# The last output store of a fused FFN kernel: waited for behind the block's end barrier, and issued in two halves from two engines

## The chip, the cores and the metric

The kernel runs on one core of one Trainium2 chip. Its time is the device time of one execution in microseconds; lower is better. The profile is a hardware trace of one execution, and its "span" runs from the first to the last recorded instruction of the program.

## What is computed

For eight images x of 1024 x 512 (float32) a reaction-diffusion step gives y, and y goes through a feed-forward layer whose two weight matrices get a per-image rank-structured addition:

```python
du_dt = zX * lap_x(y) + zY * lap_y(y) + zR * y * (1 - y)          # per image
h   = einsum('bsd,hd->bsh', du_dt, W1) + scale * einsum('bsd,bhd->bsh', du_dt, m1) + b1
h   = gelu(h)
out = x + einsum('bsh,oh->bso', h, W2) + scale * einsum('bsh,boh->bso', h, m2) + b2
```

Here m1 and m2 are outer products of rows 1 to 16 of du_dt of that image. There are B = 8 images, S = 1024 rows, D = 512 input and output channels, and 2048 hidden channels. The output is 8 x 1024 x 512 float32, 16.8 MB.

## The kernel before

The work of an image b is two halves h of 512 rows. A half accumulates its second layer in four PSUM banks `po[0]` to `po[3]`, each 128 rows x 512 channels, over 16 hidden tiles. `layer2_late` (L638 to L640 are its matmuls) finishes the four banks one after the other for the last hidden tile, i = 7, and signals each with `s_l2L`.

`ev(b, h, t)` (L1348) on VectorE adds bank `po[t]` to `xr[:, t, :]`, which holds x + b2, and signals `s_ev`. `store_out(b, h, t)` (L341) on SyncE waits for that and stores the 128 x 512 tile (256 KB) to `out`; its landing adds 16 to the semaphore `d_o[t]`. The `xr` buffer is loaded again for the next half only when `d_o[0]` to `d_o[3]` have arrived.

For the last half of the last image (b = 7, h = 1) nothing follows. VectorE ends with

```python
            c21(B - 1, 7)
            glL(B - 1, 1, 7)
            for t in range(4):
                ev(B - 1, 1, t)
```

and SyncE ends with

```python
            for t in range(4):
                store_out(B - 1, 1, t)
            for t in range(4):
                e.wait_ge(d_o[t], 16 * 2 * B)
```

The last wait (L495) is inside the block, so that the barrier of the block's end starts only when the last store has landed. TensorE ends with `layer2_late(7, 1, 7)`, ScalarE with `ghL(7, 1, 7)` (L929), and GpSimd with the transfer that adds b2 into `xr` (L539).

Of the kernel before, what the change touches and what calls it, by code (L numbers as in the profile page):

```python
# [5 lines left out]
def adaln_ffn_kernel(nc: bass.Bass, xT, xs, x, xn, pk, w1, w2, b2, out):  # L6
# [3 lines left out]
    ALU = mybir.AluOpType  # L10
    ACT = mybir.ActivationFunctionType

    B, S, D = 8, 1024, 512
# [5 lines left out]
    ctx = ExitStack()  # L19
    with ctx:  # L20
        def sb(name, shape, dt=f32):
            return ctx.enter_context(nc.sbuf_tensor(name, shape, dt))

        def sems(names):
            return [ctx.enter_context(nc.semaphore(n)) for n in names.split()]
# [28 lines left out]
        xr = sb("xr", [128, 4, 512])  # L54
# [8 lines left out]
        po = [ctx.enter_context(nc.psum_tensor(f"po{t}", [128, 512], f32)) for t in range(4)]  # L63
# [16 lines left out]
        s_l2E, s_l2L = sems("s_l2E s_l2L")  # L80
# [4 lines left out]
        s_w2f, s_w2h, s_w2l, s_ev, s_scal, s_sc = sems("s_w2f s_w2h s_w2l s_ev s_scal s_sc")  # L85
# [11 lines left out]
        d_U, d_V, d_o = sems("d_U0 d_U1"), sems("d_V0 d_V1"), sems("d_o0 d_o1 d_o2 d_o3")  # L97
# [18 lines left out]
        def steps(b, h, i):  # L116
            return 16 * b + 8 * h + i + 1

        def late(b, h, i, t=0):
            return 22 * b + 11 * h + i + t + 1  # L120
# [22 lines left out]
        def evs(b, h, t):  # L143
            return 8 * b + 4 * h + t + 1
# [80 lines left out]
        def bank_of(b, h, i, lt):  # L225
            if h == 0:
                return ph[i % 2 if lt else 2 + i % 2]
            return ph[i % 4 if lt else (i + 2) % 4]

        block = ctx.enter_context(nc.Block())  # L230

        @block.sync
        def _(e):
            def load_X(b, n):
                if (b, n) > (1, 0):
                    pb, pn = (b, n - 1) if n else (b - 1, 7)
                    e.wait_ge(s_mul, at_mul(pb, pn))
                    e.wait_ge(s_mt, at_sum(pb, pn))
                e.dma_start(X[:, :, :].rearrange("p r s -> p (r s)"), xT[b, n]).then_inc(d_x[8], 16)
# [99 lines left out]
            def store_out(b, h, t):  # L339
                e.wait_ge(s_ev, evs(b, h, t))  # L340
                e.dma_start(out[b, 512 * h + 128 * t:512 * h + 128 * t + 128, :], xr[:, t, :]).then_inc(d_o[t], 16)  # L341
# [73 lines left out]
            for b in range(1, B):  # L415
# [69 lines left out]
                if b + 1 < B:  # L485
# [3 lines left out]
                    load_EB2(b + 1, 1)  # L489
                    if b + 2 < B:  # L490
                        load_X(b + 2, 2)
            for t in range(4):
                store_out(B - 1, 1, t)
            for t in range(4):
                e.wait_ge(d_o[t], 16 * 2 * B)  # L495

        @block.gpsimd
        def _(e):
# [279 lines left out]
        def _(e):  # L778
# [128 lines left out]
            def gelu_L(b, h, i):  # L907
                bank, k = bank_of(b, h, i, 1), tile_of(b, h, i, 1)
                if h == 0:
                    e.wait_ge(s_p3, pairs(b, i))  # L910
                elif b == 0:
                    e.wait_ge(s_p4, i + 1)
                else:
                    e.wait_ge(s_c21, strassen(b, i))
                e.activation(bank[:, :], bank[:, :], ACT.Gelu, bias=b1t[:, k:k + 1]).then_inc(s_actL, 1)  # L915
# [8 lines left out]
            def ghL(b, h, i):  # L924
                if h or b == 0 and i:
                    pb, p_h, pi, t = (b, h, i - 1, 0) if i else (b, 0, 7, 3)
                    e.wait_ge(s_l2L, late(pb, p_h, pi, t))
                e.wait_ge(s_actL, steps(b, h, i))
                e.activation(gh[:, 1, :], bank_of(b, h, i, 1)[:, :], ACT.Copy).then_inc(s_ghL, 1)  # L929
# [216 lines left out]
                    outer(b + 1, 2)  # L1146
            gelu_L(B - 1, 1, 7)
            ghL(B - 1, 1, 7)

        @block.vector  # L1150
        def _(e):
# [176 lines left out]
            def c21(b, i):  # L1328
                e.wait_ge(d_U[i % 2], half_of(b, i))
                e.wait_ge(s_p4, pairs(b, i))  # L1330
                Z_ = ph[i % 4]
                e.tensor_tensor(Z_[:, :], Z_[:, :], UVs[:, 1 + i % 2, :], ALU.add).then_inc(s_c21, 1)  # L1332
# [6 lines left out]
            def glL(b, h, i):  # L1339
                e.wait_ge(s_ghL, steps(b, h, i))  # L1340
                e.tensor_tensor(gl[:, 1, :], bank_of(b, h, i, 1)[:, :], gh[:, 1, :].bitcast(f32),  # L1341
                                ALU.subtract).then_inc(s_glL, 1)

            def ev(b, h, t):
                if t == 0:
                    e.wait_ge(d_xa, 16 * (2 * b + h + 1))
                e.wait_ge(s_l2L, late(b, h, 7, t))
                e.tensor_tensor(xr[:, t, :], po[t][:, :], xr[:, t, :], ALU.add).then_inc(s_ev, 1)  # L1348
# [258 lines left out]
                        mul(b + 2, (i - 4) // 2)  # L1607
            c21(B - 1, 7)
            glL(B - 1, 1, 7)
            for t in range(4):  # L1610
                ev(B - 1, 1, t)

_INS = ["xT", "xs", "x", "xn", "pk", "w1", "w2", "b2"]
# [41 lines left out]
```

## Time and profile before

| | |
|---|---|
| median of 3 runs | 1337.73 us (1337.72 to 1338.11) |
| the profiled execution's own time | 1337.8 us |
| its span | 1335.6 us |
| own time minus span | 2.2 us |
| TensorE busy | 1330.8 us of the span |
| granted TensorE clock | 1.000 |
| last matmul starts | 1331.57 us |
| last addition ends | 1332.69 us |
| last DMA-queue issue of a store starts | 1332.7 us |
| last instruction (barrier release) | 1335.6 us |

The span is covered by TensorE almost from end to end; the change touches only the last four microseconds of it. An engine's name with a q (SPq, ACTq, POOLq) is its instruction sequencer: DMA issues, semaphore waits and the barrier's instructions stand there. A store's row gives how long its issue took; "DMA to landing" is the time from the issue to the semaphore's arrival.

### The profile page before, as it was taken

What the parts mean: (1) busy time and instruction counts of PE and PEld (TensorE: products, weight loads), DVE (VectorE), ACT (ScalarE), POOL (GpSimd) and SP (SyncE); (2) the same over time, 40 slices, a digit from 0 to 9 for tenths busy, and PEclk for the clock granted to TensorE, in tenths of its full rate; (3) what the DMA queues carried; (4) which work ended last, traced back from release to release, by engine and by line L of the source; (5) the groups of instructions that cost most, each with busy time, mean ns of one, the idle gap of its engine ahead of it and who ended that gap; (6) DMA issues with size and microseconds to landing.
All of it is one profiled execution on the core that took longest, in us unless ns stands there. A gap on an engine that the chain in (4) does not pass through costs nothing.

```text
span 1335.6 us, 17133 instructions
## 1 busy us (share of the span) xinstructions
PE 1330.8 (100%) x5904; PEld 1100.7 (82%) x5904; DVE 1034.6 (77%) x1775; ACT 795.1 (60%) x1376; POOL 256.5 (19%) x258
## 2 busy tenths in 40 slices
PE   9999999999999999999999999999999999999998
PEld 7888888888888888888888888888888888888887
DVE  8878799858897688976899668996689957665343
ACT  7644567645775556754677546675467754666442
POOL 1000122301232012320132201331022310232000
PEclk9999999999999999999999999999999999999999
DMA  7764388777777577876768667786767866776661
GB/s 245 194 155 151 80 206 213 202 214 204 185 207 200 184 213 198 208 192 200 206 189 221 181 219 191 194 218 182 222 177 215 209 183 200 162 193 162 173 196 48
DMA packets 140069, 253.51 MB, mean 190 GB/s; under 512 B 13648, under 2 KB 37456, under 8 KB 139984
## 3 DMA queue, kind: packets, MB, share of 16 engines
q1 hardware_dynamic: 121888, 200.91, 46.9%
q0 software_dynamic: 17520, 49.81, 22.2%
q10 hardware_dynamic: 576, 1.72, 0.4%
q8 instruction: 46, 0.75, 0.2%
q14 instruction: 39, 0.32, 0.1%
HBM read 189.34 MB, written 63.05 MB: 189 GB/s over the span
## 4 chain that ended last, share of the span: by engine, by line
PE 99%; DVE 0%; POOL 0%; issue 0%; DVEq 0%; POOLq 0%
PE po L640 17%; PE po L638 17%; PE po L639 17%; PE ph L624 15%; PE ph L626 15%; PE ph L622 15%; PE ph L603 1%; PE ph L632 0%; PE ph L665 0%; PE po L582 0%; PE po L696 0%; DVE xr L1348 0%; PE po L596 0%; PE ph L596 0%; PE po L588 0%; PE po L590 0%
## 5 line engine op out<-in xcount | busy, mean ns | idle before, releaser
L638 PE MATMUL po<-W2h,gh 128*128 128x512 f32 x1020 | 396.8, 389 | 0.0
L639 PE MATMUL po<-W2l,gh 128*128 128x512 f32 x1020 | 396.8, 389 | 0.0
L640 PE MATMUL po<-W2h,gl 128*128 128x512 f32 x1020 | 396.8, 389 | 0.0
L622 PE MATMUL ph<-yh,W1h 128*128 128x512 f32 x896 | 348.5, 389 | 0.0
L624 PE MATMUL ph<-yl,W1h 128*128 128x512 f32 x896 | 348.5, 389 | 0.0
L626 PE MATMUL ph<-yh,W1l 128*128 128x512 f32 x896 | 348.5, 389 | 0.0
L640 PEld LDWEIGHTS po<-W2h,gl 128*128 128x128 f32 x1020 | 191.5, 188 | 39.8
L639 PEld LDWEIGHTS po<-W2l,gh 128*128 128x128 f32 x1020 | 191.4, 188 | 39.8
L638 PEld LDWEIGHTS po<-W2h,gh 128*128 128x128 f32 x1020 | 191.4, 188 | 39.7
L622 PEld LDWEIGHTS ph<-yh,W1h 128*128 128x128 f32 x896 | 168.2, 188 | 35.0
L624 PEld LDWEIGHTS ph<-yl,W1h 128*128 128x128 f32 x896 | 168.2, 188 | 34.9
L626 PEld LDWEIGHTS ph<-yh,W1l 128*128 128x128 f32 x896 | 168.1, 188 | 34.9
L1336 DVE TENSOR_TENSOR gl<-ph,gh 128x512 fp32r<-128x512 f32 x128 | 87.8, 686 | 113.0 <-ACT gh L922 112.8
L526 POOL TENSOR_TENSOR Ts<-R 128x512 f32<-128x512 f32 x56 | 75.3, 1345 | 445.2 <-DVE W1l L1303 381.8
L1341 DVE TENSOR_TENSOR gl<-ph,gh 128x512 fp32r<-128x512 f32 x128 | 87.3, 682 | 81.5 <-ACT gh L929 81.4
L1284 DVE SCALAR_TENSOR_TENSOR W2s<-EB,SC,W2s 128x128 f32<-128x128 f32 x480 | 142.4, 346 | 1.0 <-DMA W2s<-in_w_dram 1.0
L915 ACT ACTIVATE ph<-ph,PK 128x512 f32<-128x512 f32 x128 | 84.1, 657 | 76.4 <-DVE ph L1332 71.9
L922 ACT ACTIVATE gh<-ph 128x512 fp32r<-128x512 f32 x128 | 76.7, 599 | 64.7 <-PE po L640 59.7
L1292 DVE TENSOR_TENSOR W2l<-W2s,W2h 128x512 fp32r<-128x512 f32 x124 | 111.7, 901 | 4.2 <-ACT W2h L879 4.1
L879 ACT ACTIVATE W2h<-W2s 128x512 fp32r<-128x512 f32 x124 | 77.9, 629 | 52.1 <-DVE W2s L1284 51.5
L905 ACT ACTIVATE ph<-ph,PK 128x512 f32<-128x512 f32 x128 | 83.8, 655 | 30.4 <-DVE ph L1326 16.0
L836 ACT ACTIVATE R<-EB,SC 128x256 f32<-128x256 f32 x240 | 101.8, 497 | 0.0
(123 smaller groups left out, 1370.9 us busy)
## 6 DMA issues: line engine op xcount, KB each, us to landing
W2s<-in_w_dram SPq DMA_DIRECT2D x124, 256.0 KB, 3.7
R<-in_w_dram POOLq DMA_DIRECT2D x62, 512.0 KB, 7.3
uv_scratch<-UVs SPq DMA_DIRECT2D x112, 256.0 KB, 4.3
UVs<-uv_scratch SPq DMA_DIRECT2D x112, 256.0 KB, 3.8
X<-in_xT_dram SPq DMA_DIRECT2D x56, 390.0 KB, 4.7
xr<-in_x_dram SPq DMA_DIRECT2D x16, 1024.0 KB, 5.5
xr<-in_b_dram POOLq DMA_DIRECT2D x16, 1024.0 KB, 10.7
out_dram<-xr SPq DMA_DIRECT2D x64, 256.0 KB, 2.1
```

The costliest lines, as they stand in the source:

```text
L622: e.matmul(bank[:, :], W1h[:, f, blk, wc], yh[:, q, c, :], start=first and c == 0, stop=False, skip_group_check=not first)
L624: e.matmul(bank[:, :], W1h[:, f, blk, wc], yl[:, q, c, :], start=False, stop=False, skip_group_check=not first)
L626: mm = e.matmul(bank[:, :], W1l[:, f, blk, wc], yh[:, q, c, :], start=False, stop=c == 1, skip_group_check=not first)
L638: e.matmul(po[t][:, :], gh[:, lt, st], W2h[:, k, :], start=i == 0 and lt == 0, stop=False)
L639: e.matmul(po[t][:, :], gh[:, lt, st], W2l[:, k, :], start=False, stop=False)
L640: return e.matmul(po[t][:, :], gl[:, lt, st], W2h[:, k, :], start=False, stop=i == NI - 1 and lt == 1)
L836: m = e.activation(to[:, 2 * h:2 * h + 2, 128 * c:128 * c + 128], row.rearrange("p (a q) -> p a q", a=2), ACT.Copy, scale=SC[:, b % 2, cd, ...
L915: e.activation(bank[:, :], bank[:, :], ACT.Gelu, bias=b1t[:, k:k + 1]).then_inc(s_actL, 1)
L1284: m = e.scalar_tensor_tensor(w, rows2(b, n // 4)[:, a, :], SC[:, b % 2, ck, 4 + a:5 + a], w, ALU.mult, ALU.add)
L1292: e.tensor_tensor(W2l[:, k, :], w2s_at(b, n), W2h[:, k, :].bitcast(f32), ALU.subtract).then_inc(s_w2l, 1)
L1336: e.tensor_tensor(gl[:, 0, :], bank_of(b, h, i, 0)[:, :], gh[:, 0, :].bitcast(f32), ALU.subtract).then_inc(s_glE, 1)
L1341: e.tensor_tensor(gl[:, 1, :], bank_of(b, h, i, 1)[:, :], gh[:, 1, :].bitcast(f32), ALU.subtract).then_inc(s_glL, 1)
```

## The change

The last store is treated apart from the others. (1) The addition of `po[3]` for b = 7, h = 1 becomes two instructions of 256 channels, each with its own increment of `s_ev`. (2) Its store becomes two stores of 128 KB (256 of the 512 channels, so 1 KB of every row instead of 2 KB): SyncE issues that of channels 0 to 255, and ScalarE that of channels 256 to 511; both increment `d_o[3]`. (3) The block is closed before SyncE waits for the landings: the waits on `d_o[0]` to `d_o[3]` are SyncE's first instructions behind the barrier, with 16 more for `d_o[3]`.

```diff
--- before.py
+++ after.py
@@ -227,7 +227,8 @@
                 return ph[i % 2 if lt else 2 + i % 2]
             return ph[i % 4 if lt else (i + 2) % 4]
 
-        block = ctx.enter_context(nc.Block())
+        program = ExitStack()
+        block = program.enter_context(nc.Block())
 
         @block.sync
         def _(e):
@@ -489,10 +490,10 @@
                     load_EB2(b + 1, 1)
                     if b + 2 < B:
                         load_X(b + 2, 2)
-            for t in range(4):
+            for t in range(3):
                 store_out(B - 1, 1, t)
-            for t in range(4):
-                e.wait_ge(d_o[t], 16 * 2 * B)
+            e.wait_ge(s_ev, evs(B - 1, 1, 3))
+            e.dma_start(out[B - 1, S - 128:S, 0:256], xr[:, 3, 0:256]).then_inc(d_o[3], 16)
 
         @block.gpsimd
         def _(e):
@@ -1146,6 +1147,8 @@
                     outer(b + 1, 2)
             gelu_L(B - 1, 1, 7)
             ghL(B - 1, 1, 7)
+            e.wait_ge(s_ev, evs(B - 1, 1, 3) + 1)
+            e.dma_start(out[B - 1, S - 128:S, 256:512], xr[:, 3, 256:512]).then_inc(d_o[3], 16)
 
         @block.vector
         def _(e):
@@ -1607,8 +1610,20 @@
                         mul(b + 2, (i - 4) // 2)
             c21(B - 1, 7)
             glL(B - 1, 1, 7)
+            for t in range(3):
+                ev(B - 1, 1, t)
+            e.wait_ge(s_l2L, late(B - 1, 1, 7, 3))
+            for a in (0, 256):
+                e.tensor_tensor(xr[:, 3, a:a + 256], po[3][:, a:a + 256], xr[:, 3, a:a + 256], ALU.add).then_inc(s_ev, 1)
+
+        program.close()
+
+
+        def stored(e):
             for t in range(4):
-                ev(B - 1, 1, t)
+                e.wait_ge(d_o[t], 16 * 2 * B + 16 * (t == 3))
+
+        stored(nc.sync)
 
 
 _INS = ["xT", "xs", "x", "xn", "pk", "w1", "w2", "b2"]
```

On VectorE, the end of the program, where `po3` is the last PSUM bank and `s_l2L` the signal of `layer2_late`. Before:

```order
L1341 TENSOR_TENSOR gl<-ph3,gh 128x512 [waits s_ghL]
L1348 TENSOR_TENSOR xr<-po0,xr 128x512 [waits s_l2L,d_xa]
L1348 TENSOR_TENSOR xr<-po1,xr 128x512 [waits s_l2L]
L1348 TENSOR_TENSOR xr<-po2,xr 128x512 [waits s_l2L]
L1348 TENSOR_TENSOR xr<-po3,xr 128x512 [waits s_l2L]
L20 UNCONDITIONAL_BRANCH
```

And in the changed kernel:

```order
L1344 TENSOR_TENSOR gl<-ph3,gh 128x512 [waits s_ghL]
L1351 TENSOR_TENSOR xr<-po0,xr 128x512 [waits s_l2L,d_xa]
L1351 TENSOR_TENSOR xr<-po1,xr 128x512 [waits s_l2L]
L1351 TENSOR_TENSOR xr<-po2,xr 128x512 [waits s_l2L]
L1617 TENSOR_TENSOR xr<-po3,xr 128x256 [waits s_l2L]
L1617 TENSOR_TENSOR xr<-po3,xr 128x256
L1619 UNCONDITIONAL_BRANCH
```

The last addition has become two; the branch is the jump out of the block.

On SyncE, the end of the program: the last loads of U and V from scratch, the output stores and the jump. Before:

```order
L290 DMA UVs<-uv_scratch 128x512 [waits s_c21,d_us]
L300 DMA UVs<-uv_scratch 128x512 [waits s_c22,d_vs]
L290 DMA UVs<-uv_scratch 128x512 [waits s_c21,d_us]
L341 DMA out_0_dram<-xr 128x512 [waits s_ev] x4
L20 UNCONDITIONAL_BRANCH [waits d_o2,d_o3,d_o1,d_o0]
```

And in the changed kernel:

```order
L291 DMA UVs<-uv_scratch 128x512 [waits s_c21,d_us]
L301 DMA UVs<-uv_scratch 128x512 [waits s_c22,d_vs]
L291 DMA UVs<-uv_scratch 128x512 [waits s_c21,d_us]
L342 DMA out_0_dram<-xr 128x512 [waits s_ev] x3
L496 DMA out_0_dram<-xr 128x256 [waits s_ev]
L1619 UNCONDITIONAL_BRANCH
```

The wait on the four landings no longer stands ahead of the jump; it follows behind the barrier, where no further instruction comes. On all engines the instructions ahead of these rows are the same, in the same order.

## Rows read from the trace of the kernel before

**Rows 1.** The page: span, busy time, TensorE clock, and the chain that ended last.
```profile
span 1335.6 us, 17133 instructions
...
PE 1330.8 (100%) x5904; PEld 1100.7 (82%) x5904; DVE 1034.6 (77%) x1775; ACT 795.1 (60%) x1376; POOL 256.5 (19%) x258
...
PE 99%; DVE 0%; POOL 0%; issue 0%; DVEq 0%; POOLq 0%
```

**Rows 2.** The stretches of the end (us, busy by engine, clock, DMA share, GB/s).
```profile
core 0: us, PE busy (x) PEld busy (x) DVE busy (x) ACT busy (x) POOL busy (x), PEclk, DMA share, GB/s
1331.40:1331.60 0.20, 0.20 (x3) 0.13 (x1) 0.20 (x1) 0.00 (x0) 0.00 (x0) 1.00 0.14 51
1331.60:1334.20 2.60, 0.36 (x2) 0.00 (x0) 1.09 (x2) 0.00 (x0) 0.00 (x0) 1.00 1.02 379
1334.20:1334.40 0.20, 0.00 (x0) 0.00 (x0) 0.00 (x0) 0.00 (x0) 0.00 (x0) 1.00 0.72 266
```

**Rows 3.** In order of time, 1329.9 to 1332: the additions, the stores' issues, the last matmul.
```profile
1330.02 2.66 DVE L1348 TENSOR_TENSOR xr<-po,xr 128x512 f32<-128x512 f32 x4 [2.15 <-PE po L640]
...
1330.74 2.30 SPq L341 DMA_DIRECT2D out_dram<-xr  x4
...
1331.57 0.39 PE L640 MATMUL po<-W2h,gl 128*128 128x512 f32 x1
```

**Rows 4.** The line of the output stores, from 1325 on.
```profile
L341 SPq DMA_DIRECT2D out_dram<-xr x4: 332/335/338, 1330.7 to 1332.7; - x4
...
DMA to landing us min/median/max: 2.0/2.1/2.1
```

**Rows 5.** SyncE's last waits (L495), and what they waited for.
```profile
L495 SPq EVENT_SEMAPHORE  x2: 17/22/28, 1334.2 to 1334.8; - x2
...
SPq L495 <- DMA out_dram<-xr: 1.7, 2, 1.1
```

**Rows 6.** The line of the block's end (L20).
```profile
L20 POOLq EVENT_SEMAPHORE  x2: 17/17/17, 1335.4 to 1335.5; - x2
L20 POOLq DRAIN  x1: 11811/11811/11811, 1284.2 to 1284.2; - x1
L20 ACTq DRAIN  x1: 629/629/629, 1326.6 to 1326.6; - x1
...
L20 SPq COMPARE_BRANCH  x1: 38/38/38, 1334.9 to 1334.9; - x1
L20 SPq DRAIN  x1: 79/79/79, 1335.3 to 1335.3; - x1
L20 SPq EVENT_SEMAPHORE  x1: 17/17/17, 1335.6 to 1335.6; - x1
```

**Rows 7.** An addition of 256 channels, and the last four additions.
```profile
L1220 DVE TENSOR_TENSOR xr<-xr x1: 417/417/417, 27.2 to 27.2; 128x256 f32<-128x256 f32 x1
...
L1348 DVE TENSOR_TENSOR xr<-po,xr x4: 691/692/693, 1330.0 to 1332.0; 128x512 f32<-128x512 f32 x4
```

**Rows 8.** ScalarE's transfers of L932, at the start.
```profile
L932 ACTq DMA_DIRECT2D x<-in_xT_dram x3: 408/456/587, 0.8 to 2.2; - x3
...
DMA to landing us min/median/max: 3.8/5.6/9.1
```

**Rows 9.** The page's table of transfers: small ones on SyncE's queue.
```profile
XS<-in_xs_dram SPq DMA_DIRECT2D x7, 54.0 KB, 2.2
ep_scratch<-SS SPq DMA_DIRECT2D x1, 128.0 KB, 2.8
```

**Rows 10.** GpSimd's last transfer, from 1280 on.
```profile
L539 POOL DMA_DIRECT2D xr<-in_b_dram x1: 1301/1301/1301, 1284.2 to 1284.2; - x1
...
DMA to landing us min/median/max: 11.3/11.3/11.3
```

## The prediction

> **What bounds the kernel now.** I read the page first. TensorE is busy for 1330.8 of the span's 1335.6 us and holds 99% of the chain that ended last [rows 1], so all but the tail is paced by matmuls. The change removes no matmul and puts nothing in front of one: on every engine the order ahead of the last addition is the same. So the whole effect must come out of the stretch behind the last matmul, about 4 us, which is 0.3% of the time. I therefore read that stretch alone, in this order: the timeline, the stores' line, the transfer rate by stretches, SyncE's waits, and the line of the block's end.
>
> The last matmul starts at 1331.57. The four additions run back to back from 1330.02 for 2.66 us, so the last ends at 1332.68; the four stores are issued in 2.30 us from 1330.74, each about 0.03 us behind its addition and 0.335 us long, so the last issue starts at 1332.70 [rows 3, 4]. It takes 2.1 us to land [rows 4]: 1334.8. SyncE's last wait event stands at 1334.8 too [rows 5]. Then nothing but the block's end is left: jump at 1334.9, SyncE's DRAIN at 1335.3, GpSimd's two semaphore events at 1335.4 and 1335.5, the release at 1335.6 [rows 6]. Every other engine has been in the barrier for long: ScalarE's DRAIN began at 1326.6 and took 0.63 us, GpSimd's began at 1284.2 and took 11.8 us [rows 6]. So 0.8 us (1334.8 to 1335.6) lies behind the last landing, on SyncE's path alone.
>
> A second thing is to be seen in the stretches. From 1331.6 to 1334.2 the DMA engines are busy all the time (share 1.02) at 379 GB/s, and 266 GB/s from 1334.2 to 1334.4 [rows 2]. Summed over the three stretches, 51 x 0.2 + 379 x 2.6 + 266 x 0.2 = 1049 KB, which is the four stores (4 x 262 KB). Data starts about 0.8 us after the first issue (1330.74 to some 1331.57), is never interrupted, and ends about 1334.35; the last semaphore comes 0.45 us later. So the last store's data waits in line: it would be ready to flow at 1332.70 + 0.83 = 1333.53, but three stores of 0.69 us each (262 KB / 379 GB/s) in front of it end at 1331.57 + 2.07 = 1333.64.
>
> **The change, part by part.**
>
> *The wait behind the barrier.* It takes the four waits from in front of the jump. What then is queued behind them is nothing, and what is ahead (jump, DRAIN, GpSimd's events, release) can run while the store is under way. The last engine to arrive is now ScalarE or VectorE. VectorE's second half addition ends at 1332.84 (below), ScalarE issues from 1332.87 for 0.41 to 0.59 us [rows 8], so to 1333.46 at most; then a jump like SyncE's (1334.9 to 1335.3, 0.4 us) and SyncE's 0.3 us from DRAIN to release [rows 6] give a release at about 1334.2. This is 0.7 us ahead of the landing, and hides the barrier whole. What remains behind the landing is one semaphore wait: SyncE's took 17 to 28 ns [rows 5]; with four in a row I take 0.05 us. Instead of 0.8 us, 0.05: **-0.75 us**. If the cover were gone this would cost the 0.8 us again, no more.
>
> *The addition in halves.* A 128x256 float32 addition took 417 ns, the 128x512 one 692 ns [rows 7]. Two halves are 834 ns: the first ends at 1332.01 + 0.42 = 1332.43, the second at 1332.84. That is 0.27 us earlier and 0.14 us later than before. The row of 417 ns reads SBUF only, and no row has a half-width addition that reads PSUM; it can't be under half of 692, 0.35 us, and I keep the 0.42.
>
> *The store in halves.* Half one is issued by SyncE at 1332.46. Before it SyncE has issued three stores, the third at 1332.04 for 0.34 us, so SyncE is free in time. Its data (131 KB, 0.35 us) could flow at 1333.29 but waits for the line until 1333.64, and ends at 1333.99. Half two is issued by ScalarE at 1332.87 and could flow at 1333.70, or 1333.95 if the longer issue of ScalarE (0.587 against 0.335) is added whole; the line is free at 1333.99. So it flows from 1333.99 and ends at 1334.34, where the data ended before. The early half can't overtake and the late half isn't missed: the bytes are the same and the line is full. By this the split is worth nothing. The unknown is the price of 1 KB rows and of a second queue. From below it is 0. From above I take the only 128 KB store with 1 KB rows in the trace, 2.8 us to land [rows 9], among other traffic: 1332.87 + 2.8 = 1335.67, so +0.87 us. A 54 KB load landed in 2.2 us [rows 9], and the stores of 256 KB in 2.0 to 2.1 [rows 4]; those are the nearest rows (same place, same direction), and 1332.87 + 2.05 = 1334.92. I take **+0.1 us**: landing at 1334.9.
>
> A rule speaks against this part. First the row: the DMA share of 1.02 between 1331.6 and 1334.2 [rows 2] says that all DMA engines already work for one queue. The Trainium skill, page "DMA: Bandwidth & Descriptors", section "Rules for kernel authors", says of two transfers to halves of the partitions that they serialize on the same 16 engines, whichever engine issues them, and that issuers spread over engines bring no bandwidth; these halves are of channels, but the engines shared are the same. By that rule the split gives 0, as the sum by rows does; a reader who hoped that two queues move the last 256 KB twice as fast would write -0.35 us, and the row is against it.
>
> *Sum.* -0.75 + 0.1 = -0.65 us. The profiled execution took 1337.8 us, so 1337.15; its span becomes about 1334.95. The profiled time lies 0.07 above the median of 1337.73, so against the median the forecast is **1337.1 us**, 0.05% less. The bound for a change that a measurement can tell from none is 0.2% here, 2.7 us; the forecast is within it.
>
> **The rivals.**
>
> *A: the DRAIN waits for the transfers (gain smaller).* In rows, GpSimd's DRAIN began at 1284.2 with its last transfer's issue and took 11.8 us, until 1296.0; that transfer landed 11.3 us after its issue, at 1295.5 [rows 6, 10]. The DRAIN thus ended half a microsecond behind the landing. SyncE's own DRAIN of 0.08 us came after all had landed [rows 6], so it doesn't tell. If SyncE's and ScalarE's DRAINs held on for their stores, the barrier would start only at 1334.9 after all: with the jump hidden, release at 1335.2, time 1337.4; with half a microsecond on top, release at 1335.7 and 1337.9, no gain. Against it: GpSimd's transfers are of another kind, their issue alone took 1.3 us on the engine [rows 10] against 0.335 us of SyncE's sequencer [rows 4], so its DRAIN may end with work of its own that SyncE and ScalarE don't have. The Trainium skill, page "PSUM — Partial Sum Buffer", section "Engine vs sequencer instructions", has it that a drain waits until the engine is fully idle; it doesn't say whether a transfer under way counts.
>
> *B: the change does nothing (split eats it).* The halves land late, at 1335.67 by the 2.8 us row: the span ends at 1335.7, the time is 1337.9.
>
> *C: slower.* ScalarE's queue has moved nothing since its transfers at 0.8 to 2.2 us, and there they landed 3.8 us after issue at best and 9.1 at worst [rows 8]. At 3.8 the half lands at 1336.67 and the time is 1338.9, +1.1 us. It is slower than before from 2.75 us to landing on, and by over 0.2% only from 5.4 us. Against it: those were loads of 390 KB behind other traffic; here 131 KB follow the last of a line.
>
> *D: more is gained outside the span.* 2.2 us of the time lie outside it. Four engines now leave the program 1.4 us or more ahead of SyncE. If closing work on them was on the path before and now overlaps, up to 1 us more could go: 1336.1 to 1336.9. The trace shows nothing of that work; SyncE's own share stays behind the landing, so I hold it for unlikely.
>
> **How the numbers follow.** Forecast (1336.9 to 1337.35) 0.55; A 0.20; B 0.08; D 0.11; C 0.04; anything else, as another placement of code or data in a rebuilt program, 0.02. The runs before spread over 0.4 us, so I widen each by 0.2. The range 1336.4 to 1338.0 holds the forecast, A and B and most of D, about 0.9 in all; the forecast, A, B, D and nearly all of C stay within 2.7 us of no change. So faster by over 0.2% gets 0.02, within 0.2% gets 0.96, slower 0.02. By sign alone, a small gain is likely (0.8).
>
> **What would show each step.** Right: the last store's landing between 1334.8 and 1335.0; SyncE's, ScalarE's and GpSimd's barrier instructions before about 1334.3; the program's last instruction a SyncE wait within 0.1 us of the landing; a span near 1334.95; the transfer rate unbroken at 370 to 390 GB/s until 1334.3. A would show as DRAINs of over 1 us on SyncE and ScalarE that end with the landing. B and C would show as a landing of 2.7 us or more behind ScalarE's issue, or a fall of the rate in the last 0.7 us. D would show as an own time minus span below 2.2 us. The forecast is wrong if the span moves by more than 1 us, or anything ahead of 1330 us shifts.

## The result, and the profile after

The changed kernel takes 1336.34 us (median of 22 runs, 1335.92 to 1336.73) against 1337.86 before (22 runs, 1337.57 to 1338.38): 1.5 us less, ratio 0.9988, interval 0.9982 to 0.9993. It is a small gain, clear of zero: under the 0.2% that the prediction called no change, but more than twice the forecast 0.65 us, and 0.06 us below the lower end of the range.

The page of the profile after, its span and busy time, against [rows 1]:

```profile
span 1334.8 us, 17134 instructions
...
PE 1330.1 (100%) x5904; PEld 1100.7 (82%) x5904; DVE 1035.0 (78%) x1776; ACT 794.4 (60%) x1376; POOL 256.2 (19%) x258
```

This execution took 1336.09 us by its own time. So the span is 0.8 us shorter, and the time 1.7. The part of the time that lies outside the span has gone from 2.2 to 1.3 us. That part is the steadiest number of all: it is 1.22 to 1.32 us in each of the 22 executions of the changed kernel, and 2.11 to 2.22 us in each of the 99 executions of the kernel before that were run beside the experiments. By medians the span has gone from 1335.7 or 1335.8 us (on three chips) to 1335.1, so about 0.65 us of the gain lie inside it and 0.9 outside.

The stretches of the end, with the columns of [rows 2]:

```profile
core 0: us, PE busy (x) PEld busy (x) DVE busy (x) ACT busy (x) POOL busy (x), PEclk, DMA share, GB/s
1331.40:1331.60 0.20, 0.20 (x2) 0.00 (x1) 0.20 (x1) 0.00 (x0) 0.00 (x0) 1.00 0.60 225
1331.60:1334.20 2.60, 0.23 (x1) 0.00 (x0) 1.02 (x3) 0.00 (x0) 0.00 (x0) 1.00 1.03 371
1334.20:1334.40 0.20, 0.00 (x0) 0.00 (x0) 0.00 (x0) 0.00 (x0) 0.00 (x0) 1.00 0.59 195
1334.40:1334.60 0.20, 0.00 (x0) 0.00 (x0) 0.00 (x0) 0.00 (x0) 0.00 (x0) 1.00 0.13 41
```

The line of transfers is as full as it was: share 1.03 at 371 GB/s from 1331.6 to 1334.2 (before 1.02 at 379), then falling off.

The end in order of time (start, duration):

```profile
1330.61 1.62 SPq L342 DMA_DIRECT2D out_dram<-xr  x3
...
1331.86 0.76 DVE L1617 TENSOR_TENSOR xr<-po,xr 128x256 f32<-128x256 f32 x2
1332.32 0.42 SPq L496 DMA_DIRECT2D out_dram<-xr  x1
1332.65 0.35 ACTq L1151 DMA_DIRECT2D out_dram<-xr  x1
```

The lines of the stores, first those of SyncE (whole, then half), then ScalarE's half; each with its time to landing:

```profile
L342 SPq DMA_DIRECT2D out_dram<-xr x3: 332/337/338, 1330.6 to 1331.9; - x3
...
DMA to landing us min/median/max: 2.1/2.1/2.1
...
L496 SPq DMA_DIRECT2D out_dram<-xr x1: 416/416/416, 1332.3 to 1332.3; - x1
...
DMA to landing us min/median/max: 2.1/2.1/2.1
...
L1151 ACTq DMA_DIRECT2D out_dram<-xr x1: 353/353/353, 1332.7 to 1332.7; - x1
...
DMA to landing us min/median/max: 2.1/2.1/2.1
```

Each half takes 2.1 us to land, like a whole store [rows 4]. ScalarE's half is issued at 1332.65 and lands at about 1334.8. In this execution the last addition began at 1331.86, before at 1332.0 [rows 7]: counted from the tail's start as before, the landing would be at 1334.9.

The line of the two half additions:

```profile
L1617 DVE TENSOR_TENSOR xr<-po,xr x2: 415/420/425, 1331.9 to 1332.2; 128x256 f32<-128x256 f32 x2
```

And the line of the block's end (L1619), with the waits that now follow behind it (L1624):

```profile
L1619 POOLq EVENT_SEMAPHORE  x2: 17/17/17, 1333.2 to 1333.3; - x2
L1619 POOLq DRAIN  x1: 12513/12513/12513, 1283.9 to 1283.9; - x1
...
L1619 SPq DRAIN  x1: 137/137/137, 1332.8 to 1332.8; - x1
L1619 ACTq DRAIN  x1: 152/152/152, 1333.0 to 1333.0; - x1
L1619 SPq EVENT_SEMAPHORE  x1: 17/17/17, 1333.4 to 1333.4; - x1
...
L1624 SPq EVENT_SEMAPHORE  x2: 28/28/28, 1334.1 to 1334.8; - x2
```

SyncE's DRAIN begins at 1332.8 and takes 0.14 us, ScalarE's at 1333.0 and 0.15, both while their stores are under way. The release (the last barrier event of SyncE) stands at 1333.4, 1.4 us ahead of the landing. The last instruction of the program is SyncE's wait at 1334.8. So the barrier is hidden whole.

### The profile page after: what moved, and what is told of

The parts are those of the page before. It is cut to its first block, busy times and chain, and to the rows that moved or that the text cites. A ratio compares the mean times of both kernels' runs of the same rounds, so it can differ in the third digit from the quotient of the medians.

```text
span 1334.8 us, 17134 instructions
## 1 busy us (share of the span) xinstructions
PE 1330.1 (100%) x5904; PEld 1100.7 (82%) x5904; DVE 1035.0 (78%) x1776; ACT 794.4 (60%) x1376; POOL 256.2 (19%) x258
## 4 chain that ended last, share of the span: by engine, by line
PE 99%; DMA 1%; DVE 0%; SPq 0%; issue 0%; DVEq 0%
PE po L641 17%; PE po L639 17%; PE po L640 17%; PE ph L625 15%; PE ph L627 15%; PE ph L623 15%; DMA UVs<-in_w_dram 1%; PE ph L604 1%; PE ph L633 0%; PE po L697 0%; DVE xr L1351 0%; DVE UVs L1213 0%; PE po L597 0%; SPq L243 0%; DVE xr L1617 0%; SPq L349 0%
```

## The experiments

Each experiment lists its median and that of the kernel before, run on the same chip, and "outside": the profiled execution's own time minus its span. A profiled execution can start its tail some tenths earlier or later (its first addition stood between 1329.9 and 1330.6), so spans are compared from there or by what lies outside them. Spans are recorded to 0.1 us, so one execution gives "outside" to 0.05 us; the table in part 2 has it over all executions. The 95% intervals of the ratios are about 0.0009 to either side; differences between medians of a tenth or two are not resolved by them, and where one is used, the rows are beside it.

**1. The two parts apart.** The wait alone, which leaves the addition and the store whole (against the kernel before):

```diff
             for t in range(4):
                 store_out(B - 1, 1, t)
-            for t in range(4):
-                e.wait_ge(d_o[t], 16 * 2 * B)
...
+        program.close()
...
+        def stored(e):
+            for t in range(4):
+                e.wait_ge(d_o[t], 16 * 2 * B)
+
+        stored(nc.sync)
```

> Only the wait is moved behind the barrier; the last addition and its store stay whole. Own time minus span was 2.2 us before and is 1.3 us in the changed kernel, and its span 0.8 us shorter. Theory 1 (each engine has closing work of its own behind its last instruction; four engines now do theirs while SyncE waits, and only SyncE's is left on the path) and theory 2 (what is hidden is the fetching of code behind the barrier, while any engine waits there) both say: own time minus span 1.3, span 1334.8 to 1335.1, time 1.4 to 1.7 us below before, as the changed kernel. Rival (the split in halves brought the gain outside the span): own time minus span 2.2, time 0.7 below before.

Measured: 1336.16 us, before 1337.89 (ratio 0.9987, 0.9978 to 0.9995), span 1335.2, own time 1336.42, outside 1.2. The wait alone brings the whole gain, inside the span and outside it. The additions and stores of this run in order of time:

```profile
1330.31 2.66 DVE L1347 TENSOR_TENSOR xr<-po,xr 128x512 f32<-128x512 f32 x4 [2.15 <-PE po L639]
...
1331.03 2.30 SPq L342 DMA_DIRECT2D out_dram<-xr  x4
```

And the line of SyncE's waits behind the barrier:

```profile
L1617 SPq EVENT_SEMAPHORE  x2: 28/28/28, 1334.5 to 1335.1; - x2
```

First addition at 1330.31, last landing at 1335.1: 4.8 us, as before (1330.02 to 1334.8, [rows 3, 5]).

The split alone, with the four waits put back inside the block (against the changed kernel):

```diff
             e.dma_start(out[B - 1, S - 128:S, 0:256], xr[:, 3, 0:256]).then_inc(d_o[3], 16)
+            for t in range(4):
+                e.wait_ge(d_o[t], 16 * 2 * B + 16 * (t == 3))
...
-        stored(nc.sync)
```

> Only the addition and the store in halves; the four waits stay inside the block, ahead of the barrier. Theories 1 and 2: own time minus span 2.2, time within 0.2 us of before (the line of transfers is full: 0 to +0.1). Rival (the split brought the gain outside the span): own time minus span 1.3, time about 0.9 below before.

Measured: 1338.01 us, before 1337.89 (ratio 1.0001, 0.9992 to 1.0009), span 1335.7, own time 1337.86, outside 2.2. The line of SyncE's last waits:

```profile
L498 SPq EVENT_SEMAPHORE  x2: 17/22/28, 1334.2 to 1334.9; - x2
```

And the additions in order of time, three whole and two half:

```profile
1330.00 1.98 DVE L1353 TENSOR_TENSOR xr<-po,xr 128x512 f32<-128x512 f32 x3 [2.15 <-PE po L643]
...
1331.97 0.76 DVE L1619 TENSOR_TENSOR xr<-po,xr 128x256 f32<-128x256 f32 x2
```

The landing now stands 4.9 us behind the first addition (1330.00 to 1334.9), a tenth later than with whole stores. The split brings nothing and has no part in what went outside the span.

**2. Who waits behind the barrier.** The changed kernel, with the waits run on other engines:

```diff
         stored(nc.sync)
+        stored(nc.tensor)
+        stored(nc.vector)
+        stored(nc.scalar)
+        stored(nc.gpsimd)
```

> The changed kernel, but behind the barrier all five engines wait for the four landings, so that all leave the program together again, though each has stood behind the barrier for over a microsecond. Theory 1 (closing work of other engines overlaps): own time minus span back at 2.2, time 1337.1 to 1337.3. Theory 2 (fetching of code is hidden by any wait behind the barrier): own time minus span stays 1.3, time as the changed kernel, 1336.3.

Measured: 1336.91 us, before 1337.89 (0.9992, 0.9984 to 1.0001), span 1335.2, own time 1337.01, outside 1.8. The result lies between the two theories: 0.5 us come back as theory 1 wants, but not all 0.9. All engines leave together:

```profile
L1624 SPq EVENT_SEMAPHORE  x2: 28/28/28, 1334.4 to 1335.2; - x2
L1624 ACTq EVENT_SEMAPHORE  x2: 38/38/38, 1334.4 to 1335.2; - x2
L1624 POOLq EVENT_SEMAPHORE  x2: 43/43/43, 1334.4 to 1335.2; - x2
L1624 DVEq EVENT_SEMAPHORE  x2: 50/50/50, 1334.4 to 1335.2; - x2
L1624 PEldq EVENT_SEMAPHORE  x2: 51/51/51, 1334.4 to 1335.2; - x2
```

With GpSimd alone (`stored(nc.gpsimd)` in place of `stored(nc.sync)`):

> The changed kernel, but GpSimd in SyncE's place waits for the landings behind the barrier. Theory 1: own time minus span is GpSimd's own closing work, which can be anything from SyncE's 1.3 or less up to 2.2 if GpSimd's is the longest of the five (time 1336.3 to 1337.2). Theory 2: it doesn't matter which engine waits, 1.3 and 1336.3.

Measured: 1336.89 us, before 1337.89 (0.9992, 0.9983 to 1.0001), span 1334.9, own time 1336.65, outside 1.75 (1.79 in the median of its 11 executions, the same as with all five). GpSimd alone is as slow as all five together. Its waits:

```profile
L1624 POOLq EVENT_SEMAPHORE  x2: 43/43/43, 1334.0 to 1334.8; - x2
```

The other three, each alone in SyncE's place:

> The changed kernel, but TensorE in SyncE's place waits for the landings behind the barrier. So far own time minus span was 1.2 to 1.3 us where SyncE waited alone, 1.75 where GpSimd waited alone, 1.8 where all five waited, 2.2 with no wait behind the barrier. Theory 1 (each engine has closing work of its own, and the largest of those that leave last counts): at most 1.8, some value of TensorE's own, time 1336.3 to 1336.9. Rival (GpSimd alone is special, all other engines are alike): 1.3, time 1336.3.

> The same with VectorE as the only one that waits behind the barrier. Theory 1: at most 1.8, a value of VectorE's own, time 1336.3 to 1336.9. Rival (only GpSimd is special): 1.3, time 1336.3.

> The same with ScalarE as the only one that waits behind the barrier. Theory 1: at most 1.8, a value of ScalarE's own, time 1336.3 to 1336.9. Rival (only GpSimd is special): 1.3, time 1336.3.

Measured, with the kernels where SyncE waits beside them (before was 1337.97 in the run of these three):

| waits behind the barrier | own time, span of the profiled execution | outside, median of all executions (lowest to highest) | median |
|---|---|---|---|
| SyncE (wait alone) | 1336.42, 1335.2 | 1.26 (1.22 to 1.32) | 1336.16 |
| SyncE (changed kernel) | 1336.09, 1334.8 | 1.27 (1.22 to 1.32) | 1336.34 |
| VectorE | 1336.65, 1335.3 | 1.36 (1.32 to 1.40) | 1336.40 |
| ScalarE | 1336.79, 1335.4 | 1.39 (1.34 to 1.44) | 1336.39 |
| TensorE | 1336.77, 1335.3 | 1.51 (1.47 to 1.57) | 1336.61 |
| GpSimd | 1336.65, 1334.9 | 1.79 (1.75 to 1.84) | 1336.89 |
| all five | 1337.01, 1335.2 | 1.79 (1.73 to 1.81) | 1336.91 |

Theory 1 holds: which engine leaves last decides what lies outside, GpSimd's share is the largest, and all five together cost what GpSimd costs. The rival that GpSimd alone is special and all others are alike does not fit: SyncE's medians are 1.26 to 1.29 us in four runs (parts 1, 2 and 4), those of VectorE, ScalarE and TensorE lie 0.1, 0.1 and 0.25 us over them, and another chip makes 0.02 us (before: 2.18 us on one, 2.16 on two).

**3. The 0.4 us between 2.2 and 1.8.** The kernel before, waits for the landings inside the block, and waits that are long met behind the barrier:

```diff
+        program.close()
+        def passed(e):
+            for k in range(64):                     # 16 or 32 in the later two
+                e.wait_ge(d_o[k % 4], 16 * (k // 4 + 1))
+        passed(nc.sync)                             # and the other four
```

> The kernel before (waits for the landings inside the block, undivided store), but behind the barrier all five engines run 64 waits that are long met, at 28 to 51 ns for two of them some 0.9 us on SyncE and 1.6 us on TensorE and VectorE; span 1336.5 to 1337.3. It asks about the 0.4 us between 2.2 (no wait behind the barrier) and 1.8 (all five wait). Theory 2a (that part is the fetching of code behind the barrier, hidden as soon as any time is spent there): own time minus span 1.8. Rival (it depends on the landing, not on code): 2.2.

Measured: 1340.86 us, before 1337.97 (1.0023, 1.0014 to 1.0032), span 1339.5, own time 1340.97, outside 1.5. The waits cost about twice what their rows' durations say, since there is as long a gap between them:

```profile
L1619 SPq EVENT_SEMAPHORE  x32: 27/28/28, 1336.0 to 1337.9; - x32
L1619 ACTq EVENT_SEMAPHORE  x32: 38/38/38, 1336.0 to 1338.6; - x32
L1619 DVEq EVENT_SEMAPHORE  x32: 49/50/50, 1336.0 to 1339.1; - x32
L1619 PEldq EVENT_SEMAPHORE  x32: 51/51/51, 1336.1 to 1339.4; - x32
L1619 POOLq EVENT_SEMAPHORE  x32: 42/43/43, 1336.2 to 1338.9; - x32
```

So the engines no longer left together, and the expectation's numbers were off: TensorE was last at 1339.5, and 1.5 us is its share from the table above. This holds for seven of the ten executions (1.47 to 1.55 us outside); in the other three 1.8 to 2.2 us lay outside, and no row shows why. The run doesn't decide on the 0.4 us by itself; GpSimd left at 1338.9, so its share can't be over 2.0 to 2.1 here.

On GpSimd alone, 32 of them:

> The kernel before, but GpSimd alone runs 32 waits that are long met behind the barrier; 64 took 2.7 us on it, so 32 take about 1.4 us and its last instruction stands near 1336.9 to 1337.0. Its closing work was 1.75 us where it had waited behind the barrier, and 2.2 us lie behind the span before, where it hadn't. Theory 2a (0.4 us of the 2.2 are a first fetch of code behind the barrier, which time spent there hides): own time minus span 1.8, time 1338.7 to 1338.8. Rival (the 0.4 us are there at every end that follows at once on the landing): own time minus span 2.2, time 1339.2.

Measured: 1339.27 us, before 1337.95 (1.0009, 1.0001 to 1.0018), span 1337.5, own time 1339.27, outside 1.8. The part outside is as theory 2a has it, 1.75 to 1.86 us in all 11 executions. The median is 0.5 over the expected time, since the span is 0.5 longer than expected: 0.2 is this execution's later tail (release at 1335.8 instead of 1335.6), and the rest is a gap ahead of GpSimd's first wait, which the expectation left out. The release, then GpSimd's waits:

```profile
L1614 POOLq EVENT_SEMAPHORE  x2: 17/17/17, 1335.7 to 1335.7; - x2
...
L1614 SPq EVENT_SEMAPHORE  x1: 17/17/17, 1335.8 to 1335.8; - x1
...
L1619 POOLq EVENT_SEMAPHORE  x16: 42/43/43, 1336.1 to 1337.4; - x16
```

GpSimd's last barrier event is at 1335.7 and its first instruction behind it at 1336.1. In the run where all five engines go on, the barrier ends at 1335.9:

```profile
L1614 POOLq EVENT_SEMAPHORE  x2: 17/17/17, 1335.8 to 1335.9; - x2
...
L1614 SPq EVENT_SEMAPHORE  x1: 17/17/17, 1335.9 to 1335.9; - x1
```

There the first waits of SyncE, ScalarE and VectorE stand at 1336.0, TensorE's at 1336.1 and GpSimd's at 1336.2 (rows above). So GpSimd loses 0.3 to 0.4 us between the barrier and whatever follows. That those 0.4 us stand outside the span where the program ends at the barrier, and make 2.2 of 1.8, is argued from this sum, since no row shows GpSimd's step behind the last instruction. Where the landing is waited for behind the barrier, they are over before it: the release is at 1333.4 there.

What fills them is open. A fetch of code was the guess of theory 2a, and the trace has the transfers that load instructions. The two lines are of the run on GpSimd alone. In the gap, 1335.74 to 1336.13, there is no transfer of any kind; behind it, 1336.13 to 1336.6, there is one of instructions, which begins when the gap is over:

```profile
DMA packets 0, 0.00 MB, mean 0 GB/s; under 512 B 0, under 2 KB 0, under 8 KB 0
...
q14 instruction: 1, 0.01, 4.8%
```

So no transfer fills the gap; a fetch that needs none is not excluded. Nor does what lies outside the span go by the number of such transfers: behind the last instruction of the profiled execution stand two of them in the kernel before, one in the changed kernel and none where GpSimd waits, with 2.2, 1.3 and 1.8 us outside.

On SyncE alone, 16 of them:

> The kernel before, whole store and landing waited for inside the block, but SyncE alone runs 16 waits that are long met behind the barrier; 64 took 1.9 us on it, so 16 take 0.5 us and the span grows by as much, to about 1336.1. Theory 1 (closing work of each engine, 1.2 to 1.3 us on SyncE, and the longest chain of the five sets the end, 2.2 us behind the release): SyncE is done at 1336.1 + 1.3 = 1337.4, ahead of the others at 1337.8, so the time does not change (within 0.1). Rival (SyncE's last instruction is what the end counts from, whatever the others do): +0.5 us, 1338.4.

Measured: 1338.10 us (1337.84 to 1338.89), before 1337.95 (1.0001, 0.9992 to 1.0010). The release and SyncE's waits:

```profile
L1614 POOLq EVENT_SEMAPHORE  x2: 17/17/17, 1336.0 to 1336.1; - x2
...
L1614 SPq EVENT_SEMAPHORE  x1: 17/17/17, 1336.1 to 1336.1; - x1
...
L1619 SPq EVENT_SEMAPHORE  x8: 27/28/28, 1336.2 to 1336.6; - x8
```

SyncE is busy until 1336.7, over half a microsecond behind the release at 1336.1. The own time is 1338.33, 2.2 us behind the release, as before (1337.8 and 1335.6). So work on SyncE alone behind the barrier is covered by the longer closing work of another engine, by the table GpSimd's. The medians differ by 0.15, where 0.1 was expected at most and the rival wanted 0.5; the interval holds zero.

**4. The two best, on one chip.**

> The changed kernel once more, on one chip with the next. Both theories: 1336.35, 1.5 us below before, own time minus span 1.3.

> Only the wait behind the barrier, store and addition whole, on one chip with the changed kernel. If the split costs what it cost with the wait inside the block (its landing 4.9 us behind the first addition's start instead of 4.8, time +0.1), this is 0.1 to 0.2 us faster than the changed kernel: 1336.2. If the split helps, 0.1 slower or more.

Measured: the changed kernel 1336.36 us (1336.22 to 1336.52; outside 1.3), the wait alone 1336.24 (1336.04 to 1336.53; outside 1.2), before 1337.95. In the earlier runs, which were not made side by side, they stood at 1336.34 and 1336.16. Both times the difference of 0.1 to 0.2 has the sign and about the size of the later landing, but the intervals of the times can't resolve it. The landing can be told apart: from the start of the first addition to the last landing it is 4.80 to 4.81 us in the six traces with a whole store, and 4.88 to 4.92 us in the eight with halves. The version with the wait alone is at least as fast, and simpler.

## Why the prediction was right or wrong

**The step that failed** is the one that took the time outside the span as fixed: "so 1337.15; its span becomes about 1334.95" adds the 2.2 us of before to the new span. It was weighed only as rival D (0.11, "up to 1 us more could go"), with the reason "SyncE's own share stays behind the landing, so I hold it for unlikely". The share that stays is SyncE's, but the one that was paid before was GpSimd's, and they differ: 1.3 against 1.8 us, and GpSimd has 0.4 more from the release to its next step, 2.2 in all. In the changed kernel GpSimd is released at 1333.4, so its 2.2 us end at 1335.6, ahead of SyncE's at 1336.1, and no longer count. The term missing from the sum is 1.3 - 2.2 = -0.9 us. With it: -0.75 + 0.1 - 0.9 = -1.55, and -1.52 was measured. For the wait alone -1.65, and -1.73 and -1.71 were measured. The part of the sum inside the span, -0.65, came out.

**The wait behind the barrier, -0.75 us: right.** 0.8 us lay between landing and last instruction; now the last wait is the last instruction, and with the wait alone the median span is 0.8 us shorter (1334.9 and 1335.0 against 1335.7 and 1335.8). The cover was larger than worked out: release at 1333.4 instead of 1334.2. ScalarE's issue took 0.35 us instead of 0.41 to 0.59, and the jump's 0.4 us did not occur: DRAIN followed within 0.05 us on the issue on SyncE and ScalarE. Why the jump costs 0.4 us where it follows the waits, and almost nothing where it follows an issue, is open.

**The addition in halves: mis-sized, with no effect.** Each takes 0.42 us as taken, but the second begins before the first has ended, so the pair takes 0.76 us (L1617 in the timeline above), not 0.83.

**The store in halves, +0.1 us: right, though the size was a choice between 0 and 0.87 us and no sum.** The landing came about 0.08 us later behind the first addition in the eight traces with halves, and the line of transfers is full in either kernel. Where the 0.08 us come from was not measured apart. The Trainium skill, page "DMA: Bandwidth & Descriptors", section "Rules for kernel authors", says of halves of the partitions that they share the same DMA engines and gain nothing; these halves of the channels agree with it, 1338.01 against 1337.89 us.

**Rival A fell.** SyncE's DRAIN took 0.14 us with its store under way. GpSimd's took 12.5 us, until 1296.4, with its last transfer landed 12.0 us after the issue at 1283.9: again it ends half a microsecond behind the landing. So the prediction's reading of that DRAIN was right, but it held for GpSimd's transfer alone. **Rival B and C fell:** ScalarE's first transfer in 1330 us landed in 2.1 us. **Rival D is what happened**, on top of the forecast. (Its "1.4 us or more ahead of SyncE" doesn't follow from the prediction's own sum, which has 0.7 us; 1.4 us is what was measured.)

**Open:** what each engine does in its share outside the span is not recorded, and a constant part of it may lie ahead of the first instruction. That it differs by engine is measured; what the work is, is not. The Trainium skill, page "Runtime: NRT & Kernel Launch", section "The ~15µs preamble/postamble breakdown", lists behind a kernel a barrier over all engines of about 1.5 us, a reset of semaphores by each engine of about 1.5 us, and a further barrier with a reset of the DMA rings of about 2 us. That there is work by engine agrees with the table above; the sizes don't, since the first two alone would be 3 us, where the runs have 1.3 to 2.2 us outside the span, and no run shows which of them the time takes in.

## What to carry to other kernels

The end of a program is a race of five engines, and what is waited for last should be waited for by the engine that has least to do afterwards (SyncE here), behind every barrier. A span that ends at the last recorded instruction is not the time: when a change alters which engine leaves last, check what lies outside the span before holding it fixed. A tail whose transfers already fill the DMA engines isn't shortened by cutting its last store or by a second issuer.

## What was not expected of the hardware

- The time outside the span depends on who leaves last: 1.3 us for SyncE, 1.35 for VectorE, 1.4 for ScalarE, 1.5 for TensorE, 1.8 for GpSimd.
- GpSimd's first instruction behind the barrier came 0.3 to 0.4 us after its last barrier event, SyncE's within 0.1 us; no transfer ran in that gap.
- GpSimd's DRAIN at the block's end ended 0.5 us behind the landing of its last transfer (11.8 us long before, 12.5 after); SyncE's and ScalarE's took 0.14 and 0.15 us with their stores still under way.
- Two additions of 128x256 out of PSUM, 415 and 425 ns long, took 0.76 us together.
- 64 met waits, two to an instruction, took 1.9 us on SyncE, 2.6 on ScalarE, 2.7 on GpSimd, 3.1 on VectorE and 3.3 on TensorE: 60 to 105 ns for a pair.
